# Jumping over the large-score part of attention engine after engine instead of on all engines at once

## What is computed

```python
qkv = jnp.einsum('bsd,de->bse', x, Wqkv)
q, k, v = jnp.split(qkv, 3, axis=-1)
q = _layernorm_scale_only(q, q_ln_scale)
k = _layernorm_scale_only(k, k_ln_scale)
scores = jnp.einsum('bshd,bthd->bhst', q / jnp.sqrt(jnp.float32(HEAD_DIM)), k)
scores = jnp.where(causal, NEG_INF, scores)
attn = jax.nn.softmax(scores, axis=-1)
ctx = jnp.einsum('bhst,bthd->bshd', attn, v)
out = jnp.einsum('bsd,de->bse', ctx.reshape(B, S, D_MODEL), out_W)
...
x = _layernorm(x + attention(x))
x = _layernorm(x + ffn(x))          # ffn: silu(x Wg') * (x Wu'), times Wd'
```

## Time and profile before

| | us |
|---|---|
| median of three runs | 2370.82 |
| their range | 2368.36 to 2372.70 |
| the profiled execution, its own time | 2370.67 |
| its span, first to last instruction | 2368.9 |
| the flag is written | 330.75 |
| first score on TensorE | 336.29 |
| first exponential on ScalarE | 337.61 |
| last score and sum of attention, begin of `finish` | about 1536 |

### The profile page before, as it was taken

One profiled execution on the slowest core, in us unless ns is written; L12 is line 12 of the kernel. 1 busy time (PEld: TensorE's weight loads), 2 busy tenths in 40 slices (PEclk: granted clock), 3 DMA queues, 4 the chain that ended last, 5 costly groups with the idle time before them and its releaser, 6 DMA issues. The chain is left out here.

```text
span 2368.9 us, 34364 instructions
## 1 busy us (share of the span) xinstructions
PE 2308.9 (97%) x12556; PEld 1424.3 (60%) x12578; DVE 1775.2 (75%) x1821; ACT 1291.7 (55%) x1631; POOL 245.3 (10%) x269
## 2 busy tenths in 40 slices
PE   8999979999999999999999999989999999999997
PEld 7888844444444444444444444378888888888885
DVE  7777748998889988899898998945556556465554
ACT  4444458888888888888888888711111111111111
POOL 2111112110021100211002110000000000000000
PEclk9999979999999999999999999989999999999998
DMA  7767785100821008210082101441111021110100
GB/s 252 254 238 252 231 255 106 33 23 6 179 56 33 24 6 170 60 33 24 6 165 64 33 24 41 147 151 36 36 36 54 22 69 36 37 54 18 36 19 18
DMA packets 126303, 197.50 MB, mean 83 GB/s; under 512 B 14489, under 2 KB 39577, under 8 KB 126113
## 3 DMA queue, kind: packets, MB, share of 16 engines
q1 hardware_dynamic: 126128, 195.25, 29.4%
HBM read 122.83 MB, written 72.37 MB: 82 GB/s over the span
## 5 line engine op out<-in xcount | busy, mean ns | idle before, releaser
L1041 ACT ACTIVATE probs<-score 128x1024 f32<-128x1024 f32 (+3 forms) x1152 | 1000.2, 970 | 176.1 <-PE score L953 174.6
L1104 DVE TENSOR_TENSOR total<-total,probs 128x2048 f32<-128x2048 f32 (+3 forms) x468 | 983.2, 2101 | 79.3 <-POOL probs L915 22.1
L953 PE MATMUL score<-queries,keys 98*128 98x512 f32 (+3 forms) x2304 | 641.7, 406 | 12.1 <-ACTq L1025 6.2
L953 PEld LDWEIGHTS score<-queries,keys 98*128 98x128 f32 x2304 | 380.9, 189 | 434.2 <-ACT probs L1041 350.3
L1416 ACT ACTIVATE hidden<-slot,gate_scale_sb 128x512 f32<-128x512 f32 x128 | 88.2, 689 | 633.8 <-PE slot L1352 633.8
L969 PE MATMUL ctx_acc<-probs,values 128*32 128x512 f32 (+3 forms) x3584 | 421.6, 561 | 0.0
L1478 DVE SCALAR_TENSOR_TENSOR hidden<-slot,up_scale_sb,hidden 128x512 f32<-128x512 f32 x128 | 96.0, 750 | 252.9 <-ACT hidden L1416 252.9
L915 POOL TENSOR_SCALAR_AFFINE_SELECT probs<-probs 128x512 f32<-128x512 f32 x128 | 167.3, 1308 | 1010.3 <-ACT probs L1041 1010.3
L1352 PE MATMUL slot<-xt_hi,w_front 128*128 128x512 f32 x608 | 238.5, 392 | 1.5 <-DVE xt_lo L1519 1.5
L1352 PE MATMUL slot<-xt_lo,w_front 128*128 128x512 f32 x608 | 238.1, 392 | 0.0
L969 PEld LDWEIGHTS ctx_acc<-probs,values 128*32 128x32 f32 x3584 | 85.5, 109 | 193.6 <-issue 148.6
(11 more groups left out here) (121 smaller groups left out, 2199.6 us busy)
## 6 DMA issues: line engine op xcount, KB each, us to landing
keys<-k_hi SPq DMA_DIRECT2D x64, 256.0 KB
queries<-q_hi SPq DMA_DIRECT2D x64, 256.0 KB
wq_int<-in_wq SPq DMA_DIRECT2D x48, 256.0 KB, 3.2
wq_float<-wq_f SPq DMA_DIRECT2D x48, 256.0 KB, 2.8
x_raw<-in_x_t SPq DMA_DIRECT2D x32, 256.0 KB, 3.7
v_rows<-v_out SPq DMA_DIRECT2D x32, 256.0 KB, 2.5
q_hi<-part_hi SPq DMA_DIRECT2D x32, 256.0 KB, 2.6
q_lo<-part_lo SPq DMA_DIRECT2D x32, 256.0 KB, 2.8
```

Source lines behind the costliest of these rows:

```text
L953: ins = pe.matmul(score[u % RING][:, i, cut(t):], keys[0:ROWS, kb // ST, h, kb % ST * P:(kb % ST + 1) * P], queries[0:ROWS, q_buffer[ch], ...
L1041: act.activation(probs[:, t % PB, 2 * p:2 * p + 2, cut(t):], score[u % RING][:, :, cut(t):], ACT.Exp).then_inc(exped, 1)
L1104: dve.tensor_tensor(into, into, now, ALU.add).then_inc(added, 1)
```

## The change

Two semaphores are added, `pe_in` and `act_in`. ScalarE waits for `pe_in` before its branch, which TensorE increments as the first thing behind its own jump. VectorE and GpSimd wait for `act_in` before their branches, which ScalarE increments as the first thing behind its jump. TensorE and SyncE branch as before. (Within the large-score part the increments come at its beginning.) To make room for the two, the twelve semaphores of the attention weights' loads and the twelve of the feed-forward weights' loads become one set of twelve, `weights_in`; the second user waits for 32 instead of 16.

```diff
@@ project @@
-        wqkv_in = [[sem(f"wqkv_in{dc}{m}") for m in range(3)] for dc in range(DC)]
+        wqkv_in = [keep["weights_in"][3 * dc:3 * dc + 3] for dc in range(DC)]
@@ attend @@
+        pe_in = sem("pe_in")
+        act_in = sem("act_in")
...
             general = pool.value_load(keep["flags"][0:1, 0:1], min_val=0, max_val=1)
+            pool.wait_ge(act_in, 1)
             with pool.If(general):
...
             with pe.If(general):
+                pe.sem_inc(pe_in, 1)
                 pe.sem_inc(g_read, 2)
...
                 pe.wait_ge(g_again, 16 * (3 * AHEAD + 4))
+            pe.sem_inc(pe_in, 1)
             pe.wait_ge(ones_ready, 1)
...
+            act.wait_ge(pe_in, 1)
             with act.If(general):
+                act.sem_inc(act_in, 1)
...
+            act.sem_inc(act_in, 1)
             act.sem_inc(exped, RING)
...
             dve.sem_inc(g_split, 1)
+            dve.wait_ge(act_in, 1)
             with dve.If(general):
@@ finish @@
-                            pe.wait_ge(w_in[j], 16)
+                            pe.wait_ge(w_in[j], 16 + 16)
```

More of the change, by code:

```diff
@@ L129, in weight_load @@
 def weight_load(sp, dr, keep, to, j):
-    sp.dma_start(to.bitcast(F32), dr["wq"].rearrange("(b t) p d -> b p t d", t=ST)[j]).then_inc(keep["w_in"][j], 16)
+    sp.dma_start(to.bitcast(F32), dr["wq"].rearrange("(b t) p d -> b p t d", t=ST)[j]).then_inc(keep["weights_in"][j], 16)
 def store_chunk(sp, dr, keep, g, ch):
@@ L1158, in finish @@
         y = [c.enter_context(nc.psum_tensor(f"y{st}", [P, D], F32)) for st in range(ST)]
-        w_in, small_in = keep["w_in"], keep["small_in"]
+        w_in, small_in = keep["weights_in"], keep["small_in"]
         ident_zero = sem("ident_zero")
@@ L1580, in build @@
             "gate_scale": sb("gate_scale_sb", [P, IC], F32), "up_scale": sb("up_scale_sb", [P, IC], F32),
-            "small_in": sem("small_in"), "w_in": [sem(f"w_in{j}") for j in range(BLOCKS)],
+            "small_in": sem("small_in"), "weights_in": [sem(f"weights_in{j}") for j in range(BLOCKS)],
             "ctx_in": [sem(f"ctx_in{h}") for h in range(HALF)], "x_res_in": [sem(f"x_res_in{h}") for h in range(HALF)],
```

## The result

The changed kernel takes 2374.48 us (median of 20 runs, 2371.89 to 2377.17); the kernel before, beside it, 2371.38 (20 runs, 2368.36 to 2376.03). The ratio is 1.0013, with a 95% interval of 1.0008 to 1.0019, so the change costs 3.1 us, between 1.9 and 4.5. The forecast was 2375.0, 4.2 us more than the median known then, within 0.2%. The number came out; two of its terms did not, and they partly cancelled.

The account below looks back on a forecast made before the run. TensorE, busy 97% of the span, was taken to bound the kernel, with a 4 us gap of jumps before attention. Later ScalarE and VectorE landings delay the first exponential 4.3 us, other terms 0: 2370.67 + 4.3 = 2375.0 us, range 2371.5 to 2378.0.

Parts of the forecast that it names:

- TensorE's jump, 0: Attention's beginning: TensorE's jump starts at 332.1 and lands at 335.6 us as before, neither longer nor shorter; 0 added.
- ScalarE's wait, 2.8: Attention's beginning: ScalarE's wait ends at 335.7, its jump takes 2.8 us and lands at 338.5.
- the lone jump: Reason given for ScalarE's 2.8 us: with the wait it jumps alone, where its jump among five took 3.6.
- VectorE's wait, 3.25: Attention's beginning: VectorE's wait ends at 338.6; jumping together with GpSimd takes 3.25 us, landing at 341.85 (341.4 to 342.3).
- the lone row's 2.8 and 3.7 among five: Bounds for VectorE's jump: 2.8 us from loop ends with nobody else jumping, 3.7 from its own among five; middle taken.
- SyncE, 0: Attention's beginning: SyncE doesn't wait; its second-chunk loads start just behind TensorE's landing as before; 0 added.
- The rival of dear jumps: Attention's beginning: jumps keep their 3.6 and 3.7 us; first exponential 5.6 us later, 2376.3 us in total; chance 0.28.
- There is no stage in which it waits for a load.: Rest of attention: TensorE busy 1178.87 of 1187 us, 99.3%, so what attention's beginning loses, the end loses.
- The granted clock, 0 taken, 0.95 either way: TensorE's rise from 1.2 to 2.4 GHz early in attention: 0.95 us gained or lost possible, 0 taken.
- its earlier rise: Clock rise 11.8 us after the first score, at 350.5: 2.4 us later against work 4.3 later, giving back at most 0.95.
- GpSimd's cover: First mask comes 2.1 us after the first exponential, hiding GpSimd's jump if it lands at most 2 us behind VectorE's.
- the shared semaphores: Weight loads: same transfers in the same order, feed-forward weights waited for over 1100 us later; 0 added.

Follow-up runs that it names:

- e8_sooner_and_credits: Against the kernel before: no waits, shared weight semaphores, credits ahead of the jumps, fourth chunk's queries asked for sooner; 0.9994, 2368.53 us against 2369.76.
- e11_delay_by_work: e5_queries_sooner plus 28 chained small VectorE writes ahead of its credit for the first exponential; 0.5 us under the kernel before (-2.6 to 1.7).
- e12_twice_the_delay: As e11_delay_by_work with 56 writes instead of 28; 3.6 us over the kernel before (1.4 to 5.7).
- e1_sems_alone: Kernel before with the shared weight semaphores only, no waits at the jumps; ratio 1.0002 (0.9993 to 1.0011).
- e5_queries_sooner: Kernel before with shared weight semaphores, fourth chunk's queries asked for behind that chunk's keys and values; ratio 0.9996 (0.9987 to 1.0005).
- e4_quiet_queue: Changed kernel, but SyncE holds the second chunk's loads until VectorE has landed; 1.0024 (1.0014 to 1.0035) against the kernel before.
- e10_one_jump_more: Changed kernel with the fourth chunk's queries sooner and VectorE waiting for GpSimd's landing; 10.9 us over the kernel before (7.6 to 14.0).
- e2_act_waits_alone: Changed kernel with only ScalarE's wait kept; VectorE and GpSimd jump at once; 1.0006 (0.9997 to 1.0015) against the kernel before.

## Why the number was right and two of its terms were not

- **TensorE's jump, 0.** Right: 3.53 us, and 3.4 to 4.0 in all experiments.
- **ScalarE's wait, 2.8.** The size is right: 2.77, and 2.65 to 3.0 in the seven other kernels where it waits. The reason given, the lone jump, is not shown. In e8_sooner_and_credits, e11_delay_by_work and e12_twice_the_delay all five engines jump at once, and ScalarE's jump takes 2.9 to 3.0 there too, against 3.6 to 3.7 before, in e1_sems_alone and e5_queries_sooner. Its branch and credit in e11_delay_by_work:

```profile
L1023 ACTq COMPARE_BRANCH  x1: 54/54/54, 329.7 to 329.7; - x1
...
L1031 ACTq EVENT_SEMAPHORE  x1: 17/17/17, 332.6 to 332.6; - x1
```

What made it longer in the other three stays open.

- **VectorE's wait, 3.25.** Wrong by 1.35 us. The choice between the lone row's 2.8 and 3.7 among five rested on company. The price is set by the loads: 2.98 without them in e4_quiet_queue, 4.3 to 5.0 with them in the changed kernel and three others, 9.3 in e10_one_jump_more. The step that failed stood a paragraph above, "SyncE, 0": I had its loads start on time and counted them at nothing, without asking who would now jump beside them. The earlier trace rows showed that a jump waits for packets of code, and the earlier trace rows a DMA share of 0.72 in the very stretch into which the jump was moved.
- **The rival of dear jumps.** It gave 5.6 us for the first exponential, close to the 5.7 seen, but by 3.6 and 3.7; the truth was 2.8 and 4.6. ScalarE's 2.76 in e2_act_waits_alone and VectorE's 2.98 in e4_quiet_queue speak against its cause.
- **"There is no stage in which it waits for a load."** Wrong. The 99.3% of the earlier trace rows over 1187 us hides a wait of 1.3 us. The waits of the first chunks alone, at the place where transfers that don't depend on attention's start come in, would have shown it. This is why 5.7 us at the beginning became 3.1 at the end, in part: 0.8 us in the two traces, some 2.3 where the clock falls. That the spans of these two traces differ by 3.3 us, close to the 3.1 of the medians, is chance: they make it up of 5.7 for the first exponential, less 1.9 for the earlier barrier, which is scatter, less 0.6 behind the first exponential (2031.3 to 2030.7).
- **The granted clock, 0 taken, 0.95 either way.** It rose 9.9 us after the first exponential and 14.5 after the first score; before it was 10.5 and 11.8. Over all traces the rise comes 7.9 to 10.8 us behind the first exponential, but 9.2 to 22.6 behind the first score (22.6 in e10_one_jump_more). So it goes with the exponentials and not with the first score, from which the forecast counted its earlier rise. The 0.6 us sooner gave back about 0.3 us in this trace, but that is scatter: without any wait the rise came at 7.9 (e5_queries_sooner), 8.9 (e1_sems_alone) and 10.5 (before). Windows of the changed kernel around the rise, which answer to the earlier trace rows:

```profile
346.00:351.42 5.42, 5.42 (x22) 1.67 (x21) 3.82 (x3) 2.41 (x4) 2.78 (x3) 0.50 1.09 192
351.42:357.50 6.08, 6.08 (x44) 2.98 (x48) 2.69 (x2) 5.30 (x7) 1.33 (x2) 1.00 1.10 184
```

- **GpSimd's cover, the shared semaphores.** Right: the mask followed 2.1 us behind the first exponential, and e1_sems_alone shows no cost that can be told.

The forecast was 1.4 us short at the beginning and about 2.6 us over in what comes through to the end. It was right in its total by that balance, and that is luck. Of the 2.6 us the traces explain 0.8 to 2.3; the rest is no more than the result's own interval, 1.9 to 4.5, leaves open.

## What to carry to other kernels

A jump whose target is not at hand is a fetch, and its price depends on the transfers that run while it waits: 3.0 to 9.3 us here for the same jump of VectorE's. Putting such jumps in a row adds up their latencies, and a wait in front of one can move it out of a quiet stretch into a busy one. Before saying that a delay goes through whole, look for transfers that run by their own clock: the first place where the pipeline meets one can take part of the delay back, 0.8 us here. Credits that don't depend on how a branch goes belong ahead of it; moving them took back some 2.6 of the 3.1 us here while the waits stayed.

## What the runs showed of the hardware

VectorE's jump over the same part took 2.98 us with the DMA share at 0.02, 3.1 to 3.9 beside other jumps with no loads running, 4.3 to 5.0 at a share of about 1.0, and 9.3 when the loads had been running for some 6 us and went on at 1.09. GpSimd's, alone, took 4.0 us at a share of 1.01 just before that last one. The code itself is small: a single packet of 0.01 MB came in at VectorE's lone loop end, and three with 0.02 MB at the two jumps of e4_quiet_queue. What takes the time under loads is that the packets do not move: in e10_one_jump_more none did for over 6 us behind VectorE's branch. That they stand in line behind the data's packets is the likely reason; their place in the queues is not in the trace.
